# Local attention: Newton's steps for the inverse norms on GpSimd, both largest scores ahead of the scaling by the norms

## What is computed

```
q, k, v = split(shift_token(x) @ wqkv)          # 8 heads x 64 each
q = q / clip(norm(q), 1e-12) * q_scale          # norm over the 64 of a head
k = k / clip(norm(k), 1e-12) * k_scale
q, k = rotary_xpos(q, k)                        # q*cos + rotate_half(q)*sin
sim = where(mask, -big, 8 * q @ k.T)            # own window of 64 and the one before
out = softmax(sim) @ v
x = x + out @ wo
```

## Time and profile before

| | us |
|---|---|
| median of 3 runs | 2675.28 |
| profiled execution | 2677.36 |
| its span | 2675.6 |
| PE busy (matmul) | 2415.1 |
| DVE busy | 2086.3 |
| ACT busy | 1449.2 |
| POOL busy | 1164.7 |

### The profile page before, as it was taken

The page is one execution under the profiler, slowest core; times in us unless marked ns, Lnnn a source line. Parts: engine busy times, 40 slices in busy tenths (PEclk is TensorE's granted clock), DMA queues, the critical chain, the costliest instruction groups (busy, mean ns, idle before and its releaser), DMA issues.

```text
span 2675.6 us, 41301 instructions
## 1 busy us (share of the span) xinstructions
PE 2415.1 (90%) x14910; PEld 1129.3 (42%) x14910; DVE 2086.3 (78%) x3369; ACT 1449.2 (54%) x2525; POOL 1164.7 (44%) x964
## 2 busy tenths in 40 slices
PE   6799985988868977897699999999999999999897
PEld 5444434453335654566433333433343334333344
DVE  7898876427879965996588889889889988889642
ACT  5576651627646753776365555455545554555462
POOL 1111110406845531553146666566656665566630
PEclk9899987999989999999899999999999999999999
DMA  5000001010000000000100000000000000000000
GB/s 210 0 1 1 1 1 43 14 44 0 32 16 1 1 33 1 1 1 17 44 1 9 9 9 6 9 9 10 9 7 8 9 9 9 9 9 9 5 1 16
DMA packets 21128, 42.00 MB, mean 16 GB/s; under 512 B 10494, under 2 KB 12670, under 8 KB 19772
## 3 DMA queue, kind: packets, MB, share of 16 engines
q1 hardware_dynamic: 20924, 39.35, 4.2%
HBM read 34.90 MB, written 4.45 MB: 15 GB/s over the span
## 4 chain that ended last, share of the span: by engine, by line
PE 67%; DVE 22%; issue 5%; ACT 3%; POOL 1%; DMA 0%; DVEq 0%; POOLq 0%; ACTq 0%; SPq 0%
PE PS L2663 16%; PE PS L2654 15%; PE PS L1227 6%; PE PS L2626 5%; DVE WK L2179 2%; DVE NR L274 2%; PE PS L671 2%; PE PS L672 2%; PE PS L673 2%; DVE NR L2867 2%; PE PS L1209 2%; DVE WK L2155 1%; DVE WK L271 1%; DVE WK L2162 1%; PE PS L2609 1%
## 5 line engine op out<-in xcount | busy, mean ns | idle before, releaser
L2769 ACT ACTIVATE WK<-PS 128x1024 f32<-128x1024 f32 x512 | 497.5, 1022 | 457.5 <-PE PS L2654 451.8
L2946 POOL TENSOR_TENSOR W<-W,WK 128x512 f32<-128x512 f32 x448 | 575.4, 1286 | 384.6 <-DVE W L2885 383.3
L2867 DVE TENSOR_REDUCE NR<-PS 128x2 f32<-128x1024 f32 x512 | 625.3, 1223 | 132.2 <-PE PS L2627 116.3
L2663 PE MATMUL PS<-WK,W 128*64 128x512 f32 x2048 | 494.2, 604 | 0.0
L2654 PE MATMUL PS<-WK 64*128 64x512 f16 (+1 forms) x4096 | 484.2, 377 | 0.6 <-issue 0.6
L2885 DVE TENSOR_TENSOR W<-W,WK 128x512 f32<-128x512 f32 x448 | 342.3, 766 | 9.1 <-ACT WK L2769 9.1
L2654 PEld LDWEIGHTS PS<-WK 64*128 64x128 f16 (+1 forms) x4096 | 199.5, 94 | 219.5 <-ACT WK L2769 6.5
L2663 PEld LDWEIGHTS PS<-WK,W 128*64 128x64 f32 x2048 | 124.2, 136 | 246.8 <-issue 168.9
L2626 PE MATMUL PS<-WK 64*128 64x512 f16 x512 | 195.6, 382 | 5.2 <-DVE NR L2867 4.7
L2627 PE MATMUL PS<-WK 64*128 64x512 f16 x512 | 195.7, 382 | 0.0
L2194 POOL TENSOR_TENSOR WK<-WK,W 128x512 f32<-128x512 f32 x64 | 113.4, 1793 | 176.0 <-DVE WK L2139 93.7
(11 more groups left out here) (370 smaller groups left out, 4330.6 us busy)
## 6 DMA issues: line engine op xcount, KB each, us to landing
XB<-l_rdens SPq DMA_DIRECT2D x62, 128.0 KB, 2.9
W<-in_mw SPq DMA_DIRECT2D x8, 512.0 KB, 12.1
W<-in_l2w SPq DMA_DIRECT2D x1, 3114.0 KB, 11.8
W<-in_f1w SPq DMA_DIRECT2D x1, 2816.0 KB, 19.0
W<-in_l3w SPq DMA_DIRECT2D x1, 2816.0 KB, 10.9
W<-in_f3w SPq DMA_DIRECT2D x1, 2816.0 KB, 9.9
W<-in_mw SPq DMA_DIRECT2D x8, 256.0 KB, 11.9
la_second_tables<-W SPq DMA_DIRECT2D x1, 2048.0 KB, 6.3
```

Source lines behind the costliest of these rows:

```text
L2663: m = e.matmul(k.PS[64 * i:64 * i + 64, 4, :], self.V[:, kt, g, :], self.PTB[kt // 2 % 2][:, kt % 2, i, :], start=kt == 0, stop=kt == NT - 1)
L2769: e.activation(self.PTB[kt // 2 % 2][:, kt % 2, :, :], self.k.PS[:, 2 * (kt % 2):2 * (kt % 2) + 2, :], ACT.Exp, scale=1.0 / 64).then_inc(s ...
L2867: e.tensor_reduce(self.PM[ji % 2][:, u // 4, :, u % 4], self.k.PS[:, bk:bk + 2, :], AX.X, ALU.max).then_inc(self.maxes.sem)
L2946: e.tensor_tensor(ac, ac, p, ALU.add).then_inc(self.acc1.sem)
```

## The change

`rsqrt` is split in two functions, `rsqrt_guess` (the shift and the first guess) and `rsqrt_newton` (the three steps); together they do what it did, and the layer norms still call them through `rsqrt`. In local attention VectorE now makes the guess only. GpSimd makes Newton's steps in a new function `pool_newton`, with four instructions a step in place of three (product, product, scale and add, product), twelve in all on tiles of 128x16, between its sine products and the products with the reciprocal sums. A new counter `newton` tells VectorE when the norms are ready; both the scaling and the next sum of squares wait for it. On VectorE the second largest score moves ahead of the scaling.

```
+def pool_newton(k, e, o, v, n, slot, step, at):
+    a, b = k.NR[:, 0, slot:slot + n], k.NR[:, 1, slot:slot + n]
+    for r in range(3):
+        e.wait_ge(*step(at + 4 * r))
         e.tensor_tensor(a, o, o, ALU.mult).then_inc(step.sem)
+        e.wait_ge(*step(at + 1 + 4 * r))
+        e.tensor_tensor(b, a, v, ALU.mult).then_inc(step.sem)
+        e.wait_ge(*step(at + 2 + 4 * r))
+        e.tensor_scalar(a, b, -0.5, 1.5, ALU.mult, ALU.add).then_inc(step.sem)
+        e.wait_ge(*step(at + 3 + 4 * r))
+        e.tensor_tensor(o, o, a, ALU.mult).then_inc(step.sem)
...
 LocalAttention:
-    STEPS = 13
+    STEPS, NEWTON = 4, 12
...
+        self.newton = k.counter("la_newton_steps", 16 * self.NEWTON)
...
 dve:
             if 2 <= i < NT + 2:
                 self.dve_top(e, i - 2, 0)
+                self.dve_top(e, i - 2, 1)
             if 1 <= i <= NT:
                 r4 = ro.rearrange("p (h d) -> p h d", h=16)
                 e.wait_ge(*self.rotsum(i))
-                e.wait_ge(*self.step(self.STEPS * i))
+                e.wait_ge(*self.newton(self.NEWTON * i))
                 e.tensor_tensor(r4, r4, self.RS.unsqueeze(2).broadcast_to([P, 16, 64]), ALU.mult).then_inc(self.rot.sem)
-            if 2 <= i < NT + 2:
-                self.dve_top(e, i - 2, 1)
...
 dve_squares:
         if t:
-            e.wait_ge(*self.step(self.STEPS * t))
+            e.wait_ge(*self.newton(self.NEWTON * t))
...
 dve_norms:
-        rsqrt(k, e, self.RS, self.SS, 16, 32, step, at + 2)
+        rsqrt_guess(k, e, self.RS, self.SS, 16, 32, step, at + 2)
...
 pool, after the two sine products:
+                e.wait_ge(*self.step(self.STEPS * i))
+                pool_newton(k, e, self.RS, self.SS, 16, 32, self.newton, self.NEWTON * t)
```

More of the change, by code:

```diff
@@ L261, in dve, with rsqrt_guess @@
             e.tensor_copy(k.XT[0:64, b * 512:(b + 1) * 512], k.bank(b % 2, p1=64)).then_inc(self.lower.sem)
-def rsqrt(k, e, o, v, n, slot, step, at):
-    a, b = k.NR[:, 0, slot:slot + n], k.NR[:, 1, slot:slot + n]
+def rsqrt_guess(k, e, o, v, n, slot, step, at):
+    a = k.NR[:, 0, slot:slot + n]
     e.wait_ge(*step(at))
@@ L271, in rsqrt, with rsqrt_newton @@
     e.tensor_scalar(o.bitcast(I32), a.bitcast(I32), -1.0, 1597463007.0, ALU.mult, ALU.add).then_inc(step.sem)
+    return at + 2
+def rsqrt_newton(k, e, o, v, n, slot, step, at):
+    a, b = k.NR[:, 0, slot:slot + n], k.NR[:, 1, slot:slot + n]
     for r in range(3):
+        e.wait_ge(*step(at + 3 * r))
+        e.tensor_tensor(a, o, o, ALU.mult).then_inc(step.sem)
+        e.wait_ge(*step(at + 1 + 3 * r))
+        e.scalar_tensor_tensor(out=b, in0=a, scalar=-0.5, in1=v, op0=ALU.mult, op1=ALU.mult).then_inc(step.sem)
         e.wait_ge(*step(at + 2 + 3 * r))
-        e.tensor_tensor(a, o, o, ALU.mult).then_inc(step.sem)
[L275 to L279, removed]
+        e.scalar_tensor_tensor(out=o, in0=b, scalar=1.5, in1=o, op0=ALU.add, op1=ALU.mult).then_inc(step.sem)
+    return at + 9
+def pool_newton(k, e, o, v, n, slot, step, at):
+    a, b = k.NR[:, 0, slot:slot + n], k.NR[:, 1, slot:slot + n]
+    for r in range(3):
+        e.wait_ge(*step(at + 4 * r))
+        e.tensor_tensor(a, o, o, ALU.mult).then_inc(step.sem)
+        e.wait_ge(*step(at + 1 + 4 * r))
[4 more added lines that the diff above has]
+        e.tensor_tensor(o, o, a, ALU.mult).then_inc(step.sem)
+def rsqrt(k, e, o, v, n, slot, step, at):
+    return rsqrt_newton(k, e, o, v, n, slot, step, rsqrt_guess(k, e, o, v, n, slot, step, at))
 class LayerNorm:
```

## The result

The changed kernel takes 2744.18 us (median of 4 runs, 2742.59 to 2748.39) against 2675.92 us: slower by 68.3 us, ratio 1.0254, 95% interval 1.0241 to 1.0266. The forecast was 2735 us, slower by 60. The profiled execution took 2742.59 us, its span 2740.7 us.

The account below looks back on a forecast made before the run. Rounds had VectorE busiest (11.58 of 11.97 us), TensorE at 10.89 waiting for the scaling; TensorE's ring was to bind next. Order 26, ends -2 and +1, collision 13+2, clock 19+2 sum to +61 us: 2735, range 2702 to 2764.

Parts of the forecast that it names:

- TensorE's ring: Local attention's repeating round: 10.90 us of TensorE work plus a 2.26 us gap, 13.16 us at full clock.
- The gap without collision: TensorE's wait between second score product and head transposes: 2.26 us in place of 1.07.
- The order: Both largest scores ahead of VectorE's scaling: 1.19 us more a round, +26 us in 22 rounds.
- the ends of a stage: First and last rounds of each local attention stage: filling +1 us in all, last rounds -2 us in all.
- Newton on GpSimd: Twelve small GpSimd instructions, 0.22 us a product, 0.30 with the gap, 3.6 us in all, ready before the scaling.
- The collision: GpSimd's delayed sine products hold up VectorE's scaling: +13 us in 22 rounds, 2 more in filling.
- w: The scaling's wait for GpSimd in each round, ranging from 0 to 1.25 or 1.46 us, taken as 0.6.
- The clock: TensorE at half clock behind wider gaps, one round in two: 22 x 0.85 = +19 us, 2 more in filling.
- The clean ring: Rival: same order, but the scaling goes ahead of GpSimd and the clock holds; +25, 2700 us; chance 0.20.
- VectorE's relief: Rival: work taken off VectorE shortens the round if the reduction finds scores ready; -24 us, 2652; chance of faster 0.03.

Follow-up runs that it names:

- e2: Kernel before with only both largest scores moved ahead of the scaling, Newton staying on VectorE; 2719.83 us, ratio 1.0165.
- e3: Changed kernel with GpSimd's sine products waiting for the scaling of the tile before instead of the rotation's sum; 2715.07 us, ratio 1.0144.
- e8: Changed kernel with the edits of e3 and e4 together, but ten identity transposes in place of fourteen; 2705.30 us, ratio 1.0108.
- e11: Kernel before with VectorE's reciprocal that releases GpSimd's probability products moved behind Newton's steps, just ahead of the rotation's sum; 2642.66 us, ratio 0.9878.
- e1: Changed kernel with VectorE's scaling again between the two largest scores, Newton staying on GpSimd; 2691.98 us, ratio 1.0061.
- e6: Kernel before with VectorE's reciprocal that releases GpSimd's probability products moved ahead of the sum of squares; 2681.99 us, ratio 1.0015.
- e7: Kernel e1 with GpSimd's probability products waiting for the scaling; 2694.32 us, ratio 1.0066.
- e4: Changed kernel with 14 unused identity transposes in TensorE's gap ahead of the head transposes, rounds 5 to 16; 2728.14 us, ratio 1.0198.
- e5: Changed kernel with TensorE doing both score products first, then the weighing, ahead of the head transposes; 2694.14 us, ratio 1.0061.

## Why the prediction was right, step by step

*TensorE's ring.* The gap without collision was right to 0.01 us: 2.26 in e2, e3 and, less ten transposes, e8; rounds of 13.17 against 13.16. The order was given +25 with the ends of a stage and measures 28.

*Newton on GpSimd.* Right: 0.22 us a product, steps 0.3 us apart, twelve within 3.6 us behind the rotation's sum. The first is 1.12 us long, as it waits out that sum. They end 4.4 us ahead of the scaling, where 3 were forecast.

*The collision.* The mechanism was right (e3), but not the product that is met. The forecast let the sine products start 13.0 us behind the preceding scaling, so that the first would hold the next scaling for 1.1 us. They start at 12.2 (908.34 - 896.10), and the scaling meets the second. The size, w = 0.6, was a middle taken for want of a better argument, so its fit is luck; 0.71 was measured in rounds at full clock and 0.44 to 0.50 over all, since behind a half clock the products are over when the scaling comes (gap 2.26).

*The clock.* Set at one round in two and 0.85 us; measured were 13 rounds of 22, and 1.03 us a round in the first stage, 0.91 in the second. Collision and clock together were forecast at 1.45 and came to 1.47 and 1.41 us a round. That they fit so well is partly luck: the share was a guess from five gaps, and where every gap is 2.26 us it is one round in three (e2).

*The ends of a stage.* This is the part that was off, and nearly all of the missing 8 us. From the first projection to the first head transposes it takes 2.5 us more in the first stage and 3.6 in the second, not 0.6. I had not counted that Newton waits for the rotation's sum there too (0.9 us), nor that the scaling then meets the next tile's sine product (1.0 us; it lasts 2.19, at 787.05). In the second stage another 1.5 us lie ahead of the second tile's projection, where TensorE was at half clock in this execution. The next three rounds cost 2.0 and 1.9 us. The last round was to gain 1 us and cost 1.4 in the first stage: the wait of 1.36 us did go, but a stretch at half clock and a gap of 2.94 us came. In the second stage it came out even. The two stages together are 69 us longer and the span only 65, mainly because the first stage began 3 us earlier in this execution; the work ahead of it is the same.

*Rivals.* The clean ring exists (e8, 2705) but needs two edits more. VectorE's relief was worth nothing in the repeating rounds of the changed order (13.17 us in e2 and in e3). In the old order it is worth 34 us if no wait is left ahead of the transposes (e11); there it is VectorE's waits that go, with all its arithmetic left in place.

## What to carry to other kernels

Before an instruction is moved ahead of another, see what each waits for and what waits for it: here 0.9 us of reduction moved ahead of the scaling put four steps of three engines in series, in a stage whose bound, TensorE, waited only 1.07 us a round before. Taking work off the busiest engine helps only as far as the round waits for that work. And busy time can itself be waiting: two of the four microseconds taken off VectorE were waits for GpSimd's products, and moving the one instruction that released them was worth more than moving the arithmetic. Work given to another engine also delays what stands behind it in that engine's queue. A collision that is taken away at one place has to be looked for at the next (e1, e6, e7).

## What the runs showed of the hardware

In these runs VectorE instructions with two operands from SBUF, and its small scale-and-add forms, did not run beside a GpSimd instruction; each waited for the end of the one in progress, and the two engines then took turns (the scaling 1.70 us before, 1.93 in the changed kernel, 2.40 in e1, against 1.22 in e3; L271 1.32 us before against 0.17 after; GpSimd's L293 1.12 against 0.21). Reductions did run beside it: the largest score of a full tile (L2179, from PSUM) kept 0.95 us and the sum of squares 1.2 us in every run, in e6 with a probability product under way.

TensorE's clock fell to 1.2 GHz behind gaps of 2.26 us in some rounds and not in others of the same kernel, in e2 behind every third; behind gaps of 1.3 us (e1, e4, and e5's first stage) it stayed at 2.4 GHz through all repeating rounds. No run shows what decides between the rounds. The Trainium skill (TensorE: Matmul & The Clock Gate, section HAM oscillation — how this bites in real kernels) describes such a repeated fall behind waits in a loop and its price of half the throttled time. The runs agree on the price: in e2 a round of 14.55 us has a mean clock of 0.90, that is 2.9 us at half clock, and is 1.39 us longer than one of 13.16. They differ in the waits: those of the section's example are 3 to 5 us long, here 2.26 us were enough in one round of three.
